# Attention and feed-forward stack: x loaded first, weights in pieces, v's products by key block, last transposes in another bank

## The chip, the cores and the metric

One core of one Trainium2 chip runs the whole program. The metric is the device time of one execution in microseconds, the median of several runs. A profiled execution of the same program gives the trace from which all rows below are taken; its times count from the start of its span. Engines: PE (TensorE, with PEld for its weight loads), DVE (VectorE), ACT (ScalarE), POOL (GpSimd), SP (SyncE).

## The reference, cut

Two layers on x of 16 sequences, 512 tokens, 256 features. The change touches only the first attention, with 16 heads of 64 features and windows of 128 tokens that look one window back and one forward:

```python
qkv = x @ w_qkv
q, k, v = jnp.split(qkv, 3, axis=-1)
...
q = l2norm(q) * q_scale
k = l2norm(k) * k_scale
...
bq = bq * jnp.cos(qf) + rotate_half(bq) * jnp.sin(qf)
bk = bk * jnp.cos(freqs) + rotate_half(bk) * jnp.sin(freqs)
...
sim = jnp.einsum('bwid,bwjd->bwij', bq, bk)
sim = jnp.where(window_mask, NEG, sim)
attn = jax.nn.softmax(sim, axis=-1)
out = jnp.einsum('bwij,bwjd->bwid', attn, bv)
...
return out @ w_out
```

After it come a layer norm, an int8 linear layer, a second attention without softmax, and a feed-forward block with ternary weights; all of that is one later stage, the layers, which the change does not touch.

## The kernel before

A setup block (`setup_attention`) runs first, and every engine waits at its end. It loads the projection weights of 6144 columns in two chunks of 3072, forms for each a high part (`whi`, ACT) and a low part (`wlo`, POOL for chunk 0, DVE for chunk 1), and builds the rotary tables `cos` and `sin` on DVE from `trig`, `q_scale` and `k_scale`, 32 small instructions. Then `run_attention` starts: SP loads x.

A sequence has 8 pairs of heads, and a pair has 4 windows, worked off in two halves (`u` is 0 or 1) of two windows each. Each engine runs `run_halves` over all 128 pairs in a fixed order written out by hand (`pe_half`, `act_half`, `dve_half`, `pool_half`), and semaphores tie the engines together. While pair n is in its softmax, PE projects pair n + 2 (`pe_project`: six matmuls per tile of 128 tokens, three products of high and low parts for each of two chunks of x, into `pj`), transposes q and k of pair n + 1 (`pe_q_transpose`, `pe_k_transpose`, bank `qk`), and makes the scores of the next windows (`pe_scores`, banks `sc`). DVE takes the masked maximum (L476), ACT the exponential (L381), POOL the normalized weights (L568). PE transposes these (`pe_transpose_weights`, L273): head 0 of the pair into bank `tp`, head 1 into `SC[0][0]`. ACT copies head 0 (L387) and DVE head 1 (L488) to `pt`. At the start of the next pair PE multiplies them with v into `qk` (`pe_values`, L283), once both copies of window 3 are there:

```python
e.wait_ge(g['pt_act'], NW * n + NW)
e.wait_ge(g['pt_dve'], NW * n + NW)
```

The bank `qk` is shared by the transposes of x, q and k, by v's products and by the out projection (L292), which happens in pair 0 of the next sequence. Projected q and k are rotated by DVE (L453 with cos, L455 with sin, reading the two halves of a head swapped), and added by POOL (L553); POOL then scales k by its norm (L560).

Of the kernel before, what the change touches and what calls it, by code (L numbers as in the profile page):

```python
# [99 lines left out]
def setup_attention(nc, io, mem):  # L100
    s = semaphores(nc, 'set1', 'load', 'late', 'hi_act', 'zero')
    arrived = [nc.alloc_semaphore(f'set1_wqkv{c}') for c in range(DC)]
    stages = [mem['weights'][:, :], flat(mem['ot'])[:, 0:3 * HD]]
    loads = [(mem['trig'], io['trig'].rearrange('(t p) k d -> p t k d', p=P)),
        (mem['q_scale'][:, :], broadcast_rows(io['q_scale'], DH)), (mem['k_scale'][:, :],
        broadcast_rows(io['k_scale'], DH))]

    def low_part(e, c):
        e.tensor_tensor(mem['wlo'][:, c, :], stages[c], mem['whi'][:, c, :].bitcast(F32), ALU.subtract)
    with nc.Block() as block:  # L110

        @block.sync
        def _(e):
            for c in range(DC):
                e.dma_start(stages[c], io['wqkv0'][:, c, :]).then_inc(arrived[c], 16)
            e.dma_start(mem['ident'][:, :], io['ident']).then_inc(s['late'], 16)
            e.dma_start(mem['wo'][:, :, :], io['wo0'].rearrange('(c p) n -> p c n', p=P)).then_inc(s['late'], 16)
            e.wait_ge(s['late'], 32)

        @block.scalar  # L120
        def _(e):
            e.preload_act_table_set('natural_log_exp_and_others')
            for dst, src in loads:
                e.dma_start(dst, src).then_inc(s['load'], 16)
            for c in range(DC):
                e.wait_ge(arrived[c], 16)
                e.activation(mem['whi'][:, c, :], stages[c], ACT.Copy).then_inc(s['hi_act'], 1)
            e.wait_ge(s['load'], 16 * len(loads))

        @block.gpsimd  # L130
        def _(e):
            e.memset(mem['mask'][:, :], 0.0).then_inc(s['zero'], 1)
            e.memset(mem['half'][:, :], -0.5).then_inc(s['zero'], 1)
            e.wait_ge(s['zero'], 2)
            prev, nxt = (mem['mask'][:, 0:WS], mem['mask'][:, 2 * WS:3 * WS])
            e.affine_select(out=prev, in_=prev, compare_op=ALU.is_ge, fill=MASKED, base=0, pattern=[[1, WS]],
                channel_multiplier=-1)
            e.affine_select(out=nxt, in_=nxt, compare_op=ALU.is_ge, fill=MASKED, base=0, pattern=[[-1, WS]],
                channel_multiplier=1)
            e.wait_ge(s['hi_act'], 1)  # L140
            low_part(e, 0)

        @block.vector
        def _(e):
            e.wait_ge(s['load'], 16 * len(loads))
            trig = mem['trig']
            for g, (gain, scale) in enumerate(((-Q_GAIN, mem['q_scale']), (1.0, mem['k_scale']))):
                for t in range(TT):
                    for h in range(2):
                        col = (2 * g + h) * DH  # L150
                        e.scalar_tensor_tensor(mem['cos'][:, t, col:col + DH], trig[:, t, 2 * g, :], gain,
                            scale[:, :], ALU.mult, ALU.mult)
                        swapped = scale[:, :].rearrange('p (s d) -> p s d', s=2)[:, ::-1, :]
                        e.scalar_tensor_tensor(mem['sin'][:, t, col:col + DH].rearrange('p (s d) -> p s d', s=2),
                            trig[:, t, 2 * g + 1, :].rearrange('p (s d) -> p s d', s=2), gain, swapped, ALU.mult,
                            ALU.mult)
            e.wait_ge(s['hi_act'], 2)
            low_part(e, 1)
# [1678 lines left out]
```

## Time and profile before

| | |
|---|---|
| runs, median (lowest to highest) | 3140.37 us (3139.62 to 3140.78), 3 runs |
| the profiled execution | 3136.01 us |
| its span, first to last instruction | 3134.2 us |
| PE busy | 2982.0 us, 95% |
| granted TensorE clock, mean of the span; tenths in 40 slices | 0.99; 9 in all but one, which has 7 |
| DVE, ACT, POOL busy | 2369.3, 2163.6, 1658.2 us |
| v's products (L283), first and last start | 62.9 and 1935.8 us |

The attention stage fills the time up to some 1940 us, the layers the rest. PE is the busiest engine, but a busy PE is not PE at its peak, since matmuls overlap in the record; what one costs is read from the start of one to the start of the next.

### The profile page before, as it was taken

The page shows a single profiled execution, that of the slowest core. Times are in us where ns is not written, and L with a number is a line of the kernel's source. Part 1 is how long each engine was busy: PE and PEld are TensorE (multiplying, and loading weights), DVE is VectorE, ACT ScalarE, POOL GpSimd, SP SyncE. Part 2 cuts the span into 40 slices and gives each one's busy share as a digit, 9 for nine tenths or more (in the row PEclk, how much of TensorE's full clock was granted, in tenths as well). Part 3 has the DMA queues.
Part 4 walks back from the last instruction along what each step waited for, and adds up shares of the span by engine and source line. Part 5 has one row for each costly group of instructions (what it writes and reads, how often), then busy time and mean ns, then how long its engine had stood idle before and what let it go on. Part 6 is the DMA issues. An engine that isn't in the chain of part 4 may idle for free. (4 is left out here: it accounts for less than half of the span.)

```text
span 3134.2 us, 62314 instructions
## 1 busy us (share of the span) xinstructions
PE 2982.0 (95%) x21167; PEld 2488.5 (79%) x21167; DVE 2369.3 (76%) x6867; ACT 2163.6 (69%) x5662; POOL 1658.2 (53%) x2222
## 2 busy tenths in 40 slices
PE   5999999999999999999999998699999999999996
PEld 4888888888888788788788886478888888888885
DVE  5877877877877877877877875687777777777775
ACT  4766765765765766766766765477888888888884
POOL 4655654654655655655655655334555555555555
PEclk9999999999999999999999999799999999999998
DMA  2000000000000000000000000200000000000000
GB/s 83 8 15 14 15 15 15 15 15 15 15 15 15 15 15 15 15 15 8 18 18 8 15 21 23 86 8 14 14 14 15 14 21 21 14 14 14 8 14 21
DMA packets 50058, 57.63 MB, mean 18 GB/s; under 512 B 2864, under 2 KB 47936, under 8 KB 49488
## 3 DMA queue, kind: packets, MB, share of 16 engines
q1 hardware_dynamic: 47072, 51.78, 5.3%
q8 instruction: 172, 2.82, 0.4%
q10 hardware_dynamic: 2672, 1.87, 0.2%
q14 instruction: 142, 1.16, 0.1%
HBM read 36.86 MB, written 16.78 MB: 17 GB/s over the span
## 5 line engine op out<-in xcount | busy, mean ns | idle before, releaser
L568 POOL TENSOR_SCALAR a_ex<-a_ex,a_rc 128x384 f32<-128x384 f32 (+1 forms) x1024 | 533.9, 536 | 716.6 <-DVE a_rc L483 716.6
L381 ACT ACTIVATE a_ex<-a_sm,a_nm 128x384 f32<-128x384 f32 (+1 forms) x1024 | 572.1, 560 | 62.8 <-DVE a_nm L476 50.5
L476 DVE CUSTOM_DVE_ANT_0 a_sm<-sc,a_mask,a_rn 128x384 f32<-128x384 f32 (+1 forms) x1024 | 530.9, 544 | 10.5 <-PE sc L262 10.5
L387 ACT ACTIVATE a_pt<-tp 128x256 f32<-128x256 f32 (+1 forms) x512 | 220.1, 430 | 310.4 <-PE tp L273 310.4
L231 PE MATMUL pj<-a_whi,a_xhi 128*128 128x384 f32 x1024 | 397.1, 388 | 2.0 <-DVE a_rb L455 1.7
L1599 POOL TENSOR_TENSOR b_alo<-b_ring,b_ahi 128x512 fp32r<-128x512 f32 x128 | 169.6, 1325 | 411.8 <-DVE b_ring L1428 375.2
L553 POOL TENSOR_TENSOR a_qr<-a_ra,a_rb 128x256 f32<-128x256 f32 x512 | 367.8, 733 | 24.8 <-DVE a_rb L455 22.2
L262 PE MATMUL sc<-a_kT,a_qT 64*128 64x384 f32 (+1 forms) x2048 | 345.2, 455 | 1.9 <-DVE a_pt L488 0.7
L231 PE MATMUL pj<-a_whi,a_xlo 128*128 128x384 f32 x1024 | 346.1, 338 | 0.0
L231 PE MATMUL pj<-a_wlo,a_xhi 128*128 128x384 f32 x1024 | 345.2, 337 | 0.0
L488 DVE COPY a_pt<-sc 128x256 f32<-128x256 f32 (+1 forms) x512 | 251.2, 491 | 90.3 <-PE sc L273 88.8
L283 PE MATMUL qk<-a_pt,a_v 128*64 128x128 f32 x5120 | 307.8, 274 | 10.9 <-ACT a_pt L387 0.9
L283 PEld LDWEIGHTS qk<-a_pt,a_v 128*64 128x64 f32 x5120 | 280.1, 137 | 47.1 <-issue 45.1
L262 PEld LDWEIGHTS sc<-a_kT,a_qT 64*128 64x128 f32 x2048 | 176.2, 186 | 95.3 <-issue 53.3
L453 DVE TENSOR_TENSOR a_ra<-pj,a_cos 128x256 f32<-128x256 f32 x512 | 214.7, 419 | 39.5 <-ACT a_sq L366 39.4
L273 PE MATMUL tp<-s_ident,a_ex 128*128 128x128 f32 x1280 | 228.6, 277 | 9.3 <-ACT a_pt L387 8.7
L273 PE MATMUL sc<-s_ident,a_ex 128*128 128x128 f32 x1280 | 230.5, 278 | 5.6 <-DVE a_pt L488 2.5
L292 PE MATMUL qk<-a_wo,a_ot 128*128 128x256 f32 x1024 | 228.0, 381 | 1.5 <-DVE a_res L496 0.8
L292 PEld LDWEIGHTS qk<-a_wo,a_ot 128*128 128x128 f32 x1024 | 192.0, 190 | 35.1 <-issue 8.2
L455 DVE TENSOR_TENSOR a_rb<-pj,a_sin 128x256 f32<-128x256 f32 x512 | 212.4, 415 | 0.0
L1395 DVE SCALAR_TENSOR_TENSOR b_ring<-k,b_one_bk,b_ring 128x512 f32<-128x512 f32 x128 | 95.9, 749 | 153.0 <-ACT b_ring L1259 149.6
L273 PEld LDWEIGHTS tp<-s_ident,a_ex 128*128 128x128 f32 x1280 | 152.2, 141 | 61.3 <-POOL a_ex L568 46.0
(229 smaller groups left out, 7946.5 us busy)
## 6 DMA issues: line engine op xcount, KB each, us to landing
a_xin<-x SPq DMA_DIRECT2D x16, 512.0 KB, 3.9
a_xres<-x SPq DMA_DIRECT2D x16, 512.0 KB, 3.9
y<-a_res SPq DMA_DIRECT2D x16, 512.0 KB, 2.9
b_y<-y SPq DMA_DIRECT2D x16, 512.0 KB, 3.8
out<-b_y SPq DMA_DIRECT2D x15, 512.0 KB, 2.9
a_xin<-wqkv SPq DMA_DIRECT2D x8, 256.0 KB, 2.7
a_pt<-wqkv SPq DMA_DIRECT2D x1, 1536.0 KB, 6.6
a_ot<-wqkv SPq DMA_DIRECT2D x1, 1536.0 KB, 10.5
```

The source lines that it names most:

```text
L231: last = e.matmul(PJ[t % 2][:, 0:3 * PW], a[:, c, t * P:(t + 1) * P], w[:, c, p * 3 * PW:(p + 1) * 3 * PW], start=c == 0 and k == 0, stop= ...
L262: e.matmul(SC[j][h][:, 0:width], qT[par][rows(h), (w + j) * WS:(w + j + 1) * WS], kT[par][rows(h), lo * WS:(hi + 1) * WS], start=True, sto ...
L273: last = e.transpose(TPS[h][:, k * P:(k + 1) * P], ex[h][w][:, k * P:(k + 1) * P], ident[:, :])
L283: last = e.matmul(QK[rows(h), w * WS:(w + 1) * WS], v[p % 4][:, k, rows(h)], pt[h][w][:, (k - lo) * P:(k - lo + 1) * P], start=k == lo, st ...
L292: last = e.matmul(QK[:, t * DIM:(t + 1) * DIM], ot[:, c, (2 * k + t) * P:(2 * k + t + 1) * P], wo[:, c, :], start=c == 0, stop=c == HC - 1)
L381: e.activation(ex[h][w][:, 0:width], sm[h][w % 2][:, 0:width], ACT.Exp, bias=nm[:, w, h:h + 1], scale=-1.0, accum_out=rs[:, w, h:h + 1]).t ...
L387: e.activation(pt[0][w][:, 0:width], TP[:, 0:width], ACT.Copy).then_inc(g['pt_act'], 1)
L453: e.tensor_tensor(ra[:, t % 2, :], qk, mem['cos'][:, t, :], ALU.mult)
L476: e.tensor_tensor_reduce(out=sm[h][w % 2][:, 0:width], in0=SC[w % 2][h][:, 0:width], in1=mem['mask'][:, off:off + width], scale=rn[:, par, ...
L488: e.tensor_copy(pt[1][w][:, 0:width], TPS[1][:, 0:width]).then_inc(g['pt_dve'], 1)
L553: e.tensor_tensor(qr[par][:, t, :], ra[:, t % 2, :], rb[:, t % 2, :], ALU.add).then_inc(g['rot_pool'], 1)
L568: e.tensor_scalar(row, row, 0.0, rc[:, w, h:h + 1], ALU.add, ALU.mult).then_inc(g['exn_pool'], 1)
```

## The change

Four things are changed.

1. The setup block is gone. Its work is done in `run_attention`, in the engines' own streams. SP loads x of sequence 0 in two halves first. The weights come in five pieces (of pairs 0, 1, 2 and 3, 4 and 5, 6 and 7), chunk 0 on SP's queue and chunk 1 on ACT's. High and low parts are made piece by piece: pieces 0 to 2 ahead of and among the first projections, pieces 3 and 4 in pairs 0 to 2. The second half of x is transposed into `tp`. The tables are two instructions; the rotation reads them by broadcast, and POOL's addition reads the swapped halves of `rb`.
2. v's products run over blocks of keys: per block and head one matmul of 256 or 384 columns, adding into the bank, in place of one of 128 columns per window and block. `pt` is laid out by key block, so the copies write blocks of 128 columns with a step.
3. The transposes of window 3, head 1, go to `qk` where `spare(i)` says so, in all pairs of a sequence but 0 and 6, and no longer wait for DVE's copy of window 2.
4. In the second half of a pair, except of pairs 0 and 6, the last six projection matmuls come in one run behind these transposes.

```diff
-    TPS = (TP, SC[0][0])
+    def spare(i):
+        pair, w = divmod(i, NW)
+        return w == 3 and pair % PAIRS not in (0, 6)
+
+    def tp_bank(h, i):
+        return TP if h == 0 else QK if spare(i) else SC[0][0]
...
+    def pt_keys(h, k):
+        lo, hi, width = span(k)
+        off = (lo - k + 1) * WS
+        return pt[h][:, k, off:off + width]
...
+    PIECES = [[0], [1], [2, 3], [4, 5], [6, 7]]
...
+    RAW_UNDER = {0: 3, 3: 4, 4: 5}
...
+    def act_weights_high(e, k):
+        e.wait_ge(w_in[k], 16 * DC)
+        for c in range(DC):
+            e.activation(whi[:, c, piece_columns(k)], w_raw[c][:, piece_columns(k)],
+                ACT.Copy).then_inc(g['wh_act'], 1)
...
     def pe_transpose_weights(e, i, w, h, follows):
         lo, hi, width = span(w)
         e.wait_ge(g['exn_pool'], 2 * i + h + 1)
-        if due(i):
+        if due(i) and not (h and spare(i)):
             e.wait_ge(g['pt_dve' if h else 'pt_act'], i)
-        if h and w % 2 == 0 and follows:
+        if h and spare(i):
+            seq, p = divmod(i // NW, PAIRS)
+            if due(i // NW):
+                e.wait_ge(g['ot_act'], i // NW)
+            if p == 5 and seq + 1 < B:
+                e.wait_ge(g['xl_dve'], 2 * (seq + 1) + 1)
+        elif h and w % 2 == 0 and follows:
             e.wait_ge(g['sm_dve'], 2 * (i + 2) + 1)
...
-        for w in range(NW):
-            lo, hi, width = span(w)
-            for k in range(lo, hi + 1):
-                for h in range(2):
-                    last = e.matmul(QK[rows(h), w * WS:(w + 1) * WS], v[p % 4][:, k, rows(h)],
-                        pt[h][w][:, (k - lo) * P:(k - lo + 1) * P], start=k == lo, stop=k == hi)
+        for k in range(NW):
+            lo, hi, width = span(k)
+            for h in range(2):
+                last = e.matmul(QK[rows(h), lo * WS:(hi + 1) * WS], v[p % 4][:, k, rows(h)], pt_keys(h, k),
+                    start=k == 0, stop=k == NW - 1, skip_group_check=True)
...
             pe_transpose_weights(e, i + 1, w + 1, 0, at.has_next())
-            if at.has_pair(2):
+            if at.has_pair(2) and p == 0:
                 pe_project(e, seq, n + 2, pair, w + 1, 0)
             pe_transpose_weights(e, i + 1, w + 1, 1, at.has_next())
+            if at.has_pair(2) and p:
+                pe_project(e, seq, n + 2, pair, w + 1, 0)
             if at.has_pair(2):
                 pe_project(e, seq, n + 2, pair, w + 1, 1)
...
-        e.activation(pt[0][w][:, 0:width], TP[:, 0:width], ACT.Copy).then_inc(g['pt_act'], 1)
+        e.activation(pt_window(0, w), blocks(TP, w), ACT.Copy).then_inc(g['pt_act'], 1)
...
-        e.tensor_tensor(qr[par][:, t, :], ra[:, t % 2, :], rb[:, t % 2, :], ALU.add).then_inc(g['rot_pool'], 1)
+        half = 'p (h s d) -> p h s d'
+        e.tensor_tensor(qr[par][:, t, :].rearrange(half, h=4, s=2), ra[:, t % 2, :].rearrange(half, h=4, s=2),
+            rb[:, t % 2, :].rearrange(half, h=4, s=2)[:, :, ::-1, :], ALU.add).then_inc(g['rot_pool'], 1)
...
-            for m in range(2):
-                for t in range(TT):
-                    for c in range(DC):
-                        pe_project(e, 0, m, m, t, c)
+            for m, t in [(0, 0), (0, 1), (0, 2), (0, 3), (1, 0), (1, 1)]:
+                for c in range(DC):
+                    pe_project(e, 0, m, m, t, c)
             pe_q_transpose(e, 0, 0, 0)
+            for c in range(DC):
+                pe_project(e, 0, 1, 1, 2, c)
             pe_k_transpose(e, 0, 0)
+            for c in range(DC):
+                pe_project(e, 0, 1, 1, 3, c)
             pe_scores(e, 0, 0, 0, 0)
```

PE at the end of a pair (here pair 1 of sequence 0, second half; `sc<-s_ident,a_ex` are the transposes of head 1, `tp<-s_ident,a_ex` those of head 0), before:

```order
121 L273 MATMUL sc<-s_ident,a_ex 128x128 x3
122 L273 MATMUL tp<-s_ident,a_ex 128x128 x2
123 L231 MATMUL pj<-a_whi,a_xhi 128x384
124 L231 MATMUL pj<-a_wlo,a_xhi 128x384
125 L231 MATMUL pj<-a_whi,a_xlo 128x384
126 L273 MATMUL sc<-s_ident,a_ex 128x128 x2
127 L231 MATMUL pj<-a_whi,a_xhi 128x384
128 L231 MATMUL pj<-a_wlo,a_xhi 128x384
129 L231 MATMUL pj<-a_whi,a_xlo 128x384
130 L283 MATMUL qk<-a_pt,a_v 64x128 x20
```

and the same place in the changed kernel:

```order
124 L309 MATMUL sc<-s_ident,a_ex 128x128 x3
125 L309 MATMUL tp<-s_ident,a_ex 128x128 x2
126 L309 MATMUL qk<-s_ident,a_ex 128x128 x2
127 L261 MATMUL pj<-a_whi,a_xhi 128x384
128 L261 MATMUL pj<-a_wlo,a_xhi 128x384
129 L261 MATMUL pj<-a_whi,a_xlo 128x384
130 L261 MATMUL pj<-a_whi,a_xhi 128x384
131 L261 MATMUL pj<-a_wlo,a_xhi 128x384
132 L261 MATMUL pj<-a_whi,a_xlo 128x384
133 L318 MATMUL qk<-a_pt,a_v 64x256 x2
134 L318 MATMUL qk<-a_pt,a_v 64x384 x4
135 L318 MATMUL qk<-a_pt,a_v 64x256 x2
```

The last two transposes moved ahead of three projection matmuls and into `qk`; eight wide matmuls of v's products stand in place of twenty narrow ones.

ACT at the very start, before:

```order
1 L122 ACT_TABLE_LOAD
2 L124 DMA a_res<-trig 128x4x256
3 L124 DMA a_q_scale<-q_scale 128x64
4 L124 DMA a_k_scale<-k_scale 128x64
5 L127 ACTIVATE a_whi<-a_pt 128x3072
6 L127 ACTIVATE a_whi<-a_ot 128x3072
```

and in the changed kernel:

```order
1 L708 DMA s_ident<-ident 128x128
2 L177 DMA a_ot<-wqkv 128x384
3 L711 DMA a_scales<-q_scale 128x64
4 L711 DMA a_scales<-k_scale 128x64
5 L712 ACT_TABLE_LOAD
6 L177 DMA a_ot<-wqkv 128x384
7 L177 DMA a_ot<-wqkv 128x768 x3
8 L399 ACTIVATE a_xhi<-qk 128x2x256
9 L399 ACTIVATE a_xhi<-tp 128x2x256
10 L182 ACTIVATE a_whi<-a_stage 128x384
11 L182 ACTIVATE a_whi<-a_ot 128x384
```

Eight DMAs now stand ahead of ACT's first activation, and that activation is of x and no longer of the weights.

## Rows read from the trace of the kernel before

**Rows 1.** The page, part 2: PE's busy tenths in 40 slices.

```profile
PE   5999999999999999999999998699999999999996
```

**Rows 2.** Timeline from 0 to 45: start us, duration us, engine, line, instruction, idle before.

```profile
7.35 2.76 ACT L127 ACTIVATE a_whi<-a_pt 128x3072 fp32r<-128x3072 f32 x1 [5.35 <-DMA a_pt<-wqkv]
10.20 6.67 POOL L109 TENSOR_TENSOR a_wlo<-a_pt,a_whi 128x3072 fp32r<-128x3072 f32 x1 [8.21 <-ACT a_whi L127]
...
16.31 0.64 DVE L151 SCALAR_TENSOR_TENSOR a_cos<-a_res,a_q_scale 128x64 f32<-128x64 f32 x1 [16.31 <-DMA a_k_scale<-k_scale]
...
21.07 3.34 DVE L109 TENSOR_TENSOR a_wlo<-a_ot,a_whi 128x3072 fp32r<-128x3072 f32 x1
24.68 0.37 SPq L610 DMA_DIRECT2D a_xin<-x  x1
...
28.61 1.12 PE L222 MATMUL qk<-s_ident,a_xin 128*128 128x128 f32 x4 [28.61 <-DMA a_xin<-x]
29.76 0.60 ACT L360 ACTIVATE a_xhi<-qk 128x512 fp32r<-128x512 f32 x1 [15.28 <-PE qk L222]
...
31.90 0.67 PE L231 MATMUL pj<-a_whi,a_xhi 128*128 128x384 f32 x1
```

**Rows 3.** Timeline of all engines from 39 to 49.

```profile
39.79 0.73 POOL L553 TENSOR_TENSOR a_qr<-a_ra,a_rb 128x256 f32<-128x256 f32 x1 [0.60 <-DVE a_rb L455]
41.62 1.05 POOL L560 TENSOR_TENSOR a_qr<-a_qr,a_rn 128x512 f32<-128x512 f32 x1 [1.10 <-ACT a_rn L372]
...
47.77 1.35 PE L262 MATMUL sc<-a_kT,a_qT 64*128 64x256 f32 x8 [0.69 <-ACT a_kT L376]
```

**Rows 4.** Timeline of PE from 62.5 to 63.2: the first of v's products.

```profile
62.93 0.51 PE L283 MATMUL qk<-a_pt,a_v 128*64 128x128 f32 x5
```

**Rows 5.** Timeline of PE, 1000 to 1053.

```profile
1004.70 7.07 PE L292 MATMUL qk<-a_wo,a_ot 128*128 128x256 f32 x32
...
1026.98 2.40 PE L283 MATMUL qk<-a_pt,a_v 128*64 128x128 f32 x40
1029.31 1.35 PE L262 MATMUL sc<-a_kT,a_qT 64*128 64x384 f32 x8
...
1038.31 0.34 PE L231 MATMUL pj<-a_wlo,a_xhi 128*128 128x384 f32 x1
1038.48 0.33 PE L231 MATMUL pj<-a_whi,a_xlo 128*128 128x384 f32 x1
1038.82 0.41 PE L273 MATMUL sc<-s_ident,a_ex 128*128 128x128 f32 x2
...
1039.41 0.34 PE L231 MATMUL pj<-a_whi,a_xlo 128*128 128x384 f32 x1
1039.83 2.40 PE L283 MATMUL qk<-a_pt,a_v 128*64 128x128 f32 x40
```

**Rows 6.** Timeline of DVE, 1036 to 1040.

```profile
1038.11 0.56 DVE L488 COPY a_pt<-sc 128x384 f32<-128x384 f32 x1 [0.38 <-PE sc L273]
...
1039.26 0.42 DVE L488 COPY a_pt<-sc 128x256 f32<-128x256 f32 x1
```

**Rows 7.** Timeline of ACT's queue, 1958 to 1970: the eighth issue of the layers' set-up.

```profile
1964.30 2.95 ACTq L1710 DMA_DIRECT2D b_gate<-gate  x1
```

**Rows 8.** Timeline of DVE, 1047.9 to 1053.1: the last gap before 1053.

```profile
1048.06 0.17 DVE L483 RECIPROCAL a_rc<-a_rs 128x2 f32<-128x2 f32 x1 [0.76 <-ACT a_ex L381]
```

**Rows 9.** The page, part 5: DVE's rotation, plain and swapped read (busy, mean ns, idle before).

```profile
L453 DVE TENSOR_TENSOR a_ra<-pj,a_cos 128x256 f32<-128x256 f32 x512 | 214.7, 419 | 39.5 <-ACT a_sq L366 39.4
...
L455 DVE TENSOR_TENSOR a_rb<-pj,a_sin 128x256 f32<-128x256 f32 x512 | 212.4, 415 | 0.0
```

**Rows 10.** Timeline of all engines from 1041 to 1043.6.

```profile
1041.42 1.54 POOL L553 TENSOR_TENSOR a_qr<-a_ra,a_rb 128x256 f32<-128x256 f32 x2
...
1043.45 0.33 PE L242 MATMUL qk<-s_ident,a_qr 128*128 128x128 f32 x1
```

**Rows 11.** Waits of PE, 60 to 2000: us in total, times, longest.

```profile
PE qk L249 <- DVE a_qT L468: 9.3, 16, 0.6
```

More of the change, by code:

```diff
@@ L98, in broadcast_rows @@
     return ap.rearrange('(a n) -> a n', a=1).to_broadcast([P, n])
[L100 to L113, printed above, removed]
-            for c in range(DC):
[L115 to L147, printed above, removed]
-                for t in range(TT):
-                    for h in range(2):
[L150 to L158, printed above, removed]
@@ L178, in rows, with pt_window, blocks @@
         return slice(h * DH, (h + 1) * DH)
+    def pt_keys(h, k):
+        lo, hi, width = span(k)
+        off = (lo - k + 1) * WS
+        return pt[h][:, k, off:off + width]
+    def pt_window(h, w):
+        lo, hi, width = span(w)
+        first = lo * 3 * WS + (w - lo + 1) * WS
+        return pt[h].rearrange('p k n -> p (k n)')[:, first:first + (hi - lo + 1) * 2 * WS].rearrange(
+            'p (k n) -> p k n', n=2 * WS)[:, :, 0:WS]
+    def blocks(bank, w):
+        lo, hi, width = span(w)
+        return bank[:, 0:width].rearrange('p (k n) -> p k n', n=WS)
     class Half:
@@ L202, in run_halves, with piece_columns, dma_piece @@
                     body(e, Half(b, p, u, b == 0, b == B - 1))
+    PIECES = [[0], [1], [2, 3], [4, 5], [6, 7]]
+    w_in = [nc.alloc_semaphore(f'att_w_in{k}') for k in range(len(PIECES))]
+    w_raw = [mem['stage'][:, :], flat(mem['ot'])[:, 0:3 * HD]]
+    def piece_columns(k):
+        return slice(PIECES[k][0] * 3 * PW, (PIECES[k][-1] + 1) * 3 * PW)
+    RAW_UNDER = {0: 3, 3: 4, 4: 5}
+    x_first = [nc.alloc_semaphore(f'att_x_first{k}') for k in range(2)]
+    def dma_piece(e, k, c):
+        e.dma_start(w_raw[c][:, piece_columns(k)], io['wqkv0'][:, c, piece_columns(k)]).then_inc(w_in[k], 16)
@@ new lines, in dve_tables, with pair_tables @@
+    def dve_tables(e):
+        e.wait_ge(g['scale_in'], 32)
+        e.wait_ge(g['trig_in'], 16)
+        scales = mem['scales'][:, :, :].rearrange('p k d -> p (k d)').unsqueeze(1).to_broadcast([P, TT, 2 * DH])
+        for j in range(2):
+            last = e.tensor_tensor(pair_tables(mem['rot'], j), pair_tables(mem['trig'], j), scales, ALU.mult)
+        last.then_inc(g['trig_dve'], 1)
+        e.wait_ge(g['trig_dve'], 1)
+    def pair_tables(t, j):
+        return t[:, :, 2 * j:2 * j + 2, :].rearrange('p t k d -> p t (k d)')
@@ L289, in pe_out_project @@
             e.wait_ge(g['op_dve'], 2 * seq + 1)
+        elif seq == 0:
+            e.wait_ge(g['wo_in'], 16)
         for t in range(2):
@@ L439, in act_half @@
                 act_project(e, n + 2, (p + 2) % PAIRS, w)
+        if at.first and (at.at(0, 0) or at.at(2, 0)):
+            act_weights_high(e, 3 + p // 2)
         if w1_piece(at) is not None:
@@ L545, in dve_half @@
             dve_rotate(e, n + 2, w)
+        if at.first and (at.at(0, 1) or at.at(2, 1)):
+            dve_weights_low(e, 3 + p // 2)
         if not at.first:
@@ L588, in pool_half @@
             norm.rstd(e, at.b - 1)
+        if at.first and (at.at(0, 1) or at.at(2, 1)):
+            pool_weights_low(e, 3 + p // 2)
         if w1_piece(at) is not None:
@@ L716, in attention_memory @@
     mem['weights'] = sb('pt', [P, 2 * NW * 3 * WS])
-    pt = mem['weights'][:, :].rearrange('p (h w n) -> p h w n', h=2, w=NW)
-    mem['pt'] = [[pt[:, h, w, :] for w in range(NW)] for h in range(2)]
+    pt = mem['weights'][:, :].rearrange('p (h k n) -> p h k n', h=2, k=NW)
+    mem['pt'] = [pt[:, h, :, :] for h in range(2)]
     for k, n in dict(sm=2, ex=4).items():
```

118 lines of the change are left out of this document (89 added, 29 removed).

## The prediction

> **What bounds the kernel now.** I read the page first. TensorE (PE) is busy for 95% of the span, by the table; the one thin place of the attention stage is the first slice, where PE stands at 5 tenths [rows 1]. So there are two questions: what fills the first slice, and what PE waits for in the repeating pairs of heads.
>
> The timeline of the start answers the first. Nothing multiplies until 28.61. The chain is: weights land, ACT makes the high part, POOL and DVE the low parts. DVE's second one starts at 21.07, because it is queued behind the rotary tables, whose k_scale came only at 16.31, and ends at 24.41. Only behind this block does SP issue the load of x (24.68), which lands 3.9 us later; projections begin at 31.90 [rows 2]. The first product of weights and v follows at 62.93, 31.03 us after the first projection [rows 4]. Within these 31 us PE transposes q of pair 0 only behind all eight projections, though POOL ended the last rotation of that pair at 40.52 (39.79 and 0.73) and began the norm of k at 41.62; the first scores start at 47.77 [rows 3].
>
> For the second question I take one pair, from its v products at 1026.98 to the next at 1039.83, 12.85 us. PE has hardly a gap. The start of each instruction against the next shows two: the last projection matmul ahead of the last transposes has 0.34 us (1038.48 to 1038.82) where its like take 0.17, and the last one ahead of the v products 0.42 (1039.41 to 1039.83) [rows 5]. Both wait on DVE's copies. DVE does the copy of window 2 (from 1038.11, after waiting for PE's transposes of that window), then a masked maximum and a reciprocal, and at once the copy of window 3 (1039.26, 0.42 us long, so to 1039.68) [rows 6].
>
> **The change part by part.**
>
> *Start.* The separate block goes. x is loaded first, in two halves, and the weights in five pieces. The queues start at about 0.7, and a load of x takes 3.9 us from issue to the first transpose (24.68 to 28.61); a half takes less, so its transposes run from about 3.5 to 4.6, and those of the second half to 5.7 (1.12 us each) [rows 2]. ACT has eight DMAs to issue ahead of its first activation. At SP's 0.37 us each, or half a microsecond, that ends at 3.7 to 4.7; but in the layers' set-up ACT has such a series too, and its eighth issue took 2.95 us [rows 7]. Free of that ACT starts its work on x at about 5, with it at 7.5. Then come two high parts of x (0.6 each), two high parts of 384 columns (2.76/8 and a start, 0.45 each), and the low part on DVE (3.34/8 and a start, 0.45) with POOL's (6.67/8, 0.83) beside it: 2.8 us in all. First projection at 7.9 to 10.5; I take 9.2, which is 22.7 us sooner than 31.90. Bounds: 7.5, if ACT waits for nothing, and 14, if the first pieces come nearly as late as k_scale does now.
>
> *The 31 us behind it.* Two pieces of the high and low parts now stand among the first pair's work. Piece 1 puts 0.9 us on ACT and POOL and 0.45 on DVE between projections; PE's own rhythm there is about 1.4 us per tile, so little shows. Piece 2 on ACT (1.7 us) lies under the norms of DVE, on POOL (1.7) ahead of the norm of k, which starts near 42.3 instead of 41.62 on the old scale. Against it, PE transposes q before its last two projections. The first scores then come about 1.8 us earlier than by the old distance of 15.87. Pieces 3 and 4 (1.5 us of ACT, 0.9 of DVE, 1.7 of POOL, each once) fall into pairs 0 to 2, where DVE has up to 0.76 us idle in a half pair [rows 8]; I charge a third of their 4.1 us, 1.3. Net -0.5 us, bounds -2 and +4.
>
> *v's products by key block.* Now 40 instructions of 128 columns take 2.33 us (1026.98 to 1029.31). The out projection, in one stream, takes 7.07 us for 32 of 256 columns, 0.216 each once the tail is off: two clock periods per column at 2.4 GHz, the level that the table's granted clock of 9 tenths and more stands for [rows 5]. By that rate 40 of 128 columns would take 4.3 us; they take half, so the two heads, in the two halves of the array's columns, run side by side and each pair of instructions takes 0.109. The change has 16 instructions of 256 or 384 columns: the same columns. 2 x (0.216 + 0.322 + 0.322 + 0.216) = 2.15 against 20 x 0.109 = 2.19. So 0.04 us a pair, 0.07 if the skew between the heads goes too; loads are hidden now as before. Not every pair passes it on: in pair 1 of each sequence, behind the out projection, PE waits 0.6 for DVE's copy of q anyway (9.3 us in 16 times), and in two more pairs of each eight DVE works without a gap from a place like 1048.06 to the end of the pair [rows 8, 11]. Five of eight, 80 pairs: 3.2 us; bounds 0 and 9.
>
> *Last transposes through the bank of q and k, projections in one run.* The wait at 1038.82 is on DVE's copy of window 2, which still reads the old bank. With another bank it goes, and six projection matmuls follow in a run. But the v products wait for DVE's copy of window 3, which ends at 1039.68 because of what DVE does before it, and none of that waits on these transposes [rows 6]. PE saves 0.16 us ahead of a wait that grows by 0.16. Worth 0; the cover is DVE's chain from 1038.11. The same holds where DVE is busy throughout.
>
> *Access patterns.* DVE's rotation reads the tables by broadcast and no longer in swapped halves, and both copies write blocks of 128 with a step. Now a swapped read costs 415 ns and a plain one 419 [rows 9], so I take 0, at most 0.01 each. POOL's addition reads swapped halves, which no row of POOL shows; the nearest, its product with a broadcast factor, takes 1.05 us for 512 elements, less per element than the plain addition's 0.73 for 256 [rows 3, 10]. I take 0.
>
> **Sum.** -22.7 - 0.5 - 3.2 = -26.4 us on an execution of 3136.0 (span 3134.2 and 1.8 around it), so 3109.6 there. That execution is 4.4 us under the median of the three runs, 3140.4; set against the median: 3114.
>
> **The rivals.** *The reorder pays.* If the copy of window 3 is not held by DVE's queue but by the transposes, 96 pairs get back 0.16 (0.3 in some): 15 to 22 us more, 3095. For it: PE does wait at both places. Against it: DVE's gapless rows. 10%.
>
> *The start pays less.* ACT's issues block until the pieces have landed, or the tables come late as k_scale does: first projection near 17, 7.5 us less, 3122. For it: the 2.95 us. Against it: x and the first pieces stand first in both queues. 12%.
>
> *POOL's swapped read is slow.* Two additions run from 1041.42 to 1042.96, and PE wants q at 1043.45 [rows 10]; 0.49 us are spare. Beyond 0.98 us per addition each pair loses twice the excess. The gain of 26 us is gone at 1.08 us; at double time (1.47) the kernel takes 3239 (2 x 0.49 x 128 = 125 more). Against it: the broadcast row. 4%. The Trainium skill ("GPSIMD Engine Reference", section 3.1) says that addresses are generated in hardware at no cycles; by it the addition stays as it is and this rival falls, but no row here shows that for a swapped read.
>
> *The two heads no longer run side by side* with 384 columns: 2.13 us a pair, 3387. Against it: the scores, whose two heads lie in the two halves of the rows, take 1.35 us, tail included, for 8 instructions of 256 and 384 columns, which only fits side by side [rows 5]. 2%.
>
> *Fewer instructions pay by themselves.* If an instruction's 0.058 us (2.33/40) were its own cost and not its columns', the 24 that go would save 1.4 us a pair, 178 in all: 2936. Against it: the out projection's 0.216 for twice the columns fits the columns alone [rows 5]. 1%. The Trainium skill ("TensorE: Matmul & The Clock Gate", section "Back-to-back issue gap") speaks for this rival: it has sustained pairs of load and matmul at about 81 ns for 128 columns and 131 ns for 512, by which 40 instructions would take 3.2 us and 16 wide ones, interpolated, 1.7, an estimate of 197 us in all. The row's 2.33 us for the 40 does not agree with it.
>
> **How the numbers follow.** My forecast, 3114 with its own range 3105 to 3119, has 71%. The range for 8 in 10 takes in the lesser start and most of the paying reorder: 3096 to 3123. A measurement tells no change to about 0.2%, 6 us. Faster: forecast, the rivals of the reorder and the start, and the last one, 0.94. Slower: POOL and serial heads, 0.05. Same 0.01.
>
> **What would show it.** First projection at 9.2 (7.9 to 10.5), first v products at about 40; v products 2.27 to 2.30 to the scores; pair 1 still 12.8 long, the wait at the last transposes gone and that ahead of the v products about 0.5 longer than the matmul; POOL's addition 0.73. Wrong, if pairs fall to 12.6 or less, if POOL's addition passes 0.98, or if ACT's first activation comes after 9.

## The result, and the profile after

| | before | after |
|---|---|---|
| median (lowest to highest), 6 runs of each | 3139.99 us (3136.19 to 3140.94) | 3115.87 us (3114.87 to 3117.91) |
| profiled execution, span | 3136.01, 3134.2 us | 3117.74, 3115.9 us |
| first projection, first scores | 31.90, 47.77 | 10.74, 27.80 |
| first v products, last v products | 62.93, 1933.65 | 44.95, 1916.43 |

The ratio is 0.9926 [0.9913, 0.9939]: 24 us less by the medians, where 26 were forecast from 3140.4. The two traces differ by 18.3 only: the execution before was 4.4 us under the median of its first three runs, the one after is 1.9 above its own. (The last v products' start is that of their first instruction.)

The page of the changed kernel, part 2 (tenths in 40 slices), beside [rows 1]:

```profile
PE   7999999999999999999999997699999999999996
PEclk9999999999999999999999999799999999999998
```

PE's first slice went from 5 to 7. The one other digit that moved, in slice 25 (8 to 7), is where the attention stage ends. The timeline of its start, beside [rows 2] (start us, duration us, engine, line, instruction, idle before):

```profile
2.69 4.84 SPq L177 DMA_DIRECT2D a_stage<-wqkv  x4
2.71 1.28 ACT L712 ACT_TABLE_LOAD   x1 [2.71 <-issue]
2.75 4.81 ACTq L177 DMA_DIRECT2D a_ot<-wqkv  x4
...
4.02 1.11 PE L247 MATMUL qk<-s_ident,a_xin 128*128 128x128 f32 x4 [4.02 <-DMA a_xin<-x]
...
7.61 0.60 ACT L399 ACTIVATE a_xhi<-qk 128x512 fp32r<-128x512 f32 x1 [3.61 <-issue]
...
8.58 0.53 ACT L182 ACTIVATE a_whi<-a_stage 128x384 fp32r<-128x384 f32 x1
...
9.18 1.00 POOL L187 TENSOR_TENSOR a_wlo<-a_stage,a_whi 128x384 fp32r<-128x384 f32 x1 [7.21 <-ACT a_whi L182]
9.55 1.05 DVE L187 TENSOR_TENSOR a_wlo<-a_ot,a_whi 128x384 fp32r<-128x384 f32 x1
...
10.74 0.66 PE L261 MATMUL pj<-a_whi,a_xhi 128*128 128x384 f32 x1 [4.22 <-DVE a_wlo L187]
```

x is transposed from 4.02, but ACT takes it up only at 7.61: its last four issues take 4.81 us. That is the blocked issue of [rows 7], which I had counted. DVE's low part takes 1.05 us and not 0.45: it runs beside POOL's and ends 0.42 after it (10.18 to 10.60).

The same view shows the projections slow at first:

```profile
16.01 0.52 PE L261 MATMUL pj<-a_wlo,a_xhi 128*128 128x384 f32 x1
...
16.60 0.34 PE L261 MATMUL pj<-a_whi,a_xhi 128*128 128x384 f32 x1
```

Up to 16.6 a projection matmul takes 0.52 us and starts 0.32 behind the last one; from there on it takes 0.34, at 0.17. The view by stretches has PEclk 1.00 from 11 to 16, but the clock's record in this trace begins only at 16.5, and the view counts time without a record as full. The 0.52 us is what these matmuls take further down, where the record has half. So these 5.9 us are by their durations at the lower level, 1.2 GHz. The kernel before has 3.0 us of it (31.90 to 34.90).

Further down the same view, around the first scores:

```profile
19.10 1.21 DVE L503 TENSOR_REDUCE a_ss<-a_sq 128x16 f32<-128x1024 f32 x1
...
19.95 1.82 POOL L187 TENSOR_TENSOR a_wlo<-a_stage,a_whi 128x768 fp32r<-128x768 f32 x1
...
20.34 1.46 DVE L506 TENSOR_SCALAR a_ss<-a_ss 128x16 f32<-128x16 f32 x1
...
23.58 0.69 PE L261 MATMUL pj<-a_whi,a_xhi 128*128 128x384 f32 x1 [2.58 <-DVE a_rb L498]
...
27.80 1.35 PE L292 MATMUL sc<-a_kT,a_qT 64*128 64x256 f32 x8
```

A DVE instruction of 16 columns takes 1.46 us, until POOL's low part of piece 2 ends. Behind it stands both engines' work for q and k, and PE waits 2.58. Pair 0 shows the same with piece 3:

```profile
47.92 1.79 POOL L187 TENSOR_TENSOR a_wlo<-a_stage,a_whi 128x768 fp32r<-128x768 f32 x1
...
49.19 0.56 DVE L506 TENSOR_SCALAR a_ss<-a_ss 128x16 f32<-128x16 f32 x1
...
49.68 0.72 POOL L598 TENSOR_TENSOR a_qr<-a_ra,a_rb 128x256 f32<-128x256 f32 x1
...
50.45 0.97 PE L272 MATMUL qk<-s_ident,a_qr 128*128 128x128 f32 x4 [1.86 <-POOL a_qr L598]
...
51.96 0.52 PE L261 MATMUL pj<-a_wlo,a_xhi 128*128 128x384 f32 x1
```

POOL's last rotation of pair 1 stands behind 1.79 us of low part, and PE waits 1.86 for it, for which there was no wait before. The matmuls behind it take 0.52 and not 0.34. The view by stretches (PEclk is the third number from the end) says why:

```profile
50.40:53.00 2.60, 2.55 (x11) 2.55 (x12) 1.51 (x5) 1.74 (x6) 1.05 (x1) 0.55 0.00 0
53.00:55.00 2.00, 2.00 (x14) 1.85 (x13) 0.77 (x4) 1.23 (x5) 0.00 (x0) 0.73 0.00 0
55.00:57.00 2.00, 2.00 (x15) 1.69 (x15) 1.52 (x7) 1.69 (x6) 1.72 (x4) 1.00 0.00 0
```

The granted clock fell to half, the lower level of 1.2 GHz, just behind the wait, for all but the first 0.3 us of the first stretch, and was back at 2.4 GHz in the middle of the second (0.73 of 2 us is half for 1.1). Pair 2 shows the same with piece 4: a wait of 1.94 us, and half clock behind it.

The end of a repeating pair, PE, beside [rows 5]:

```profile
1023.96 0.38 PE L309 MATMUL qk<-s_ident,a_ex 128*128 128x128 f32 x2
1024.10 0.42 PE L261 MATMUL pj<-a_whi,a_xhi 128*128 128x384 f32 x1
...
1025.06 0.33 PE L261 MATMUL pj<-a_whi,a_xlo 128*128 128x384 f32 x1
1025.58 0.98 PE L318 MATMUL qk<-a_pt,a_v 128*64 128x256 f32 x6 [0.19 <-DVE a_pt L530]
```

and DVE there, beside [rows 6]:

```profile
1023.94 0.56 DVE L530 COPY a_pt<-sc 128x384 f32<-128x384 f32 x1 [0.31 <-PE sc L309]
...
1024.95 0.16 DVE L525 RECIPROCAL a_rc<-a_rs 128x2 f32<-128x2 f32 x1
1025.03 0.41 DVE L530 COPY a_pt<-qk 128x256 f32<-128x256 f32 x1
```

The wait at the transposes is gone, and that ahead of the v products is 0.52 from start to start where it was 0.42 (I had it grow by 0.16). But the copy of window 3 starts 0.08 us behind the reciprocal. Before, it started 0.14 behind it (the reciprocal of 1039.12, the copy of 1039.26), just after the transposes of 1038.82, 0.41 long, had ended. So it did wait for them, by some 0.06 us.

Two groups of the page, and the waits of PE from 60 to 2000, answer to [rows 9, 10] and [rows 11]:

```profile
L598 POOL TENSOR_TENSOR a_qr<-a_ra,a_rb 128x256 f32<-128x256 f32 x512 | 369.3, 735 | 12.2 <-DVE a_rb L498 9.0
...
L498 DVE TENSOR_TENSOR a_rb<-pj,a_rot 128x256 f32<-128x256 f32 x512 | 212.2, 414 | 0.0
```

```profile
PE qk L318 <- DVE a_pt L530: 23.9, 96, 0.6
PE qk L279 <- DVE a_qT L510: 9.8, 16, 0.7
```

POOL's swapped read costs nothing (735 ns; 733 before), DVE's reads neither, and the wait for DVE's copy of q is what it was.

### The profile page after: what moved, and what is told of

It reads as the page before. It is cut to its first block and busy times, and to the rows that moved or that the text cites. A ratio compares the mean times of both kernels' runs of the same rounds, so it can differ in the third digit from the quotient of the medians.

```text
span 3115.9 us, 56168 instructions
## 1 busy us (share of the span) xinstructions
PE 2972.7 (95%) x18095; PEld 2381.2 (76%) x18095; DVE 2360.4 (76%) x6841; ACT 2164.3 (69%) x5670; POOL 1658.1 (53%) x2226
## 5 line engine op out<-in xcount | busy, mean ns | idle before, releaser
L318 PE MATMUL qk<-a_pt,a_v 128*64 128x384 f32 (+1 forms) x2048 | 303.9, 437 | 26.1 <-DVE a_pt L530 23.9
L318 PEld LDWEIGHTS qk<-a_pt,a_v 128*64 128x64 f32 x2048 | 158.4, 136 | 153.3 <-issue 60.4
L530 DVE COPY a_pt<-sc 128x384 f32<-128x384 f32 (+1 forms) x416 | 210.1, 505 | 85.3 <-PE sc L309 84.7
L497 DVE TENSOR_TENSOR a_ra<-pj,a_rot 128x256 f32<-128x256 f32 x512 | 214.6, 419 | 40.5 <-ACT a_sq L405 39.3
L498 DVE TENSOR_TENSOR a_rb<-pj,a_rot 128x256 f32<-128x256 f32 x512 | 212.2, 414 | 0.0
L261 PEld LDWEIGHTS pj<-a_whi,a_xhi 128*128 128x128 f32 x1024 | 195.3, 191 | 9.7 <-issue 4.7
L606 POOL TENSOR_TENSOR a_qr<-a_qr,a_rn 128x512 f32<-128x512 f32 x128 | 134.5, 1051 | 120.3 <-ACT a_rn L411 120.1
```

What stands on the lines that cost most here:

```text
L318: last = e.matmul(QK[rows(h), lo * WS:(hi + 1) * WS], v[p % 4][:, k, rows(h)], pt_keys(h, k), start=k == 0, stop=k == NW - 1, skip_group_c ...
L497: e.tensor_tensor(ra[:, t % 2, :].rearrange(heads, k=2, h=2), qk, rotary(t, 0), ALU.mult)
```

## The experiments

All were timed beside the kernel before on the same chip, whose medians there were 3136.6 (e1 to e4), 3137.9 (e5 to e8) and 3138.1 (e9, e10); the changed kernel's 3115.87 stood beside 3139.99. A difference of two medians from different groups is therefore good to some 4 us only, and the times inside the traces carry the finer readings. "Pairs" are the distances from one pair's v products to the next, read as starts in the timeline; "96 pairs" is the time from the first v products of sequence 2 to those of sequence 14.

| kernel | median us | ratio [95%] | first projection | first scores | first v products | pairs 0, 1, 2, 3 | 96 pairs |
|---|---|---|---|---|---|---|---|
| before | 3139.99 | | 31.90 | 47.77 | 62.93 | 12.82 12.86 12.83 12.83 | 1427.39 |
| changed | 3115.87 | 0.9926 [0.9913, 0.9939] | 10.74 | 27.80 | 44.95 | 16.25 13.54 16.31 12.71 | 1422.08 |
| e1 start only | 3121.94 | 0.9954 [0.9941, 0.9968] | 10.93 | 28.09 | 45.30 | 14.71 13.55 14.71 12.82 | 1427.22 |
| e2 old v products | 3118.58 | 0.9943 [0.9931, 0.9956] | 10.82 | 27.55 | 44.63 | 14.65 13.55 16.31 12.75 | 1423.56 |
| e3 bank, old order | 3115.76 | 0.9934 [0.9922, 0.9947] | 10.58 | 26.19 | 43.27 | 14.64 13.54 16.31 12.71 | 1421.92 |
| e4 high, low parts later | 3109.71 | 0.9916 [0.9903, 0.9930] | 10.75 | 25.07 | 41.71 | 12.73 12.71 12.71 12.73 | 1422.03 |
| e5 POOL's alone later | 3110.84 | 0.9911 [0.9897, 0.9924] | 11.10 | 25.55 | 43.47 | 13.40 13.57 13.49 12.71 | 1422.27 |
| e6 issues on SP | 3114.89 | 0.9924 [0.9911, 0.9938] | 9.33 | 26.42 | 43.48 | 14.64 13.53 16.32 12.73 | 1421.91 |
| e7 = e4 and e6 | 3106.26 | 0.9895 [0.9881, 0.9908] | 10.39 | 24.82 | 42.42 | 12.71 12.71 12.71 12.71 | 1422.09 |
| e8 order, old bank | 3148.07 | 1.0031 [1.0020, 1.0042] | 11.27 | 27.92 | 44.81 | 15.08 13.89 14.75 13.19 | 1447.36 |
| e9 = e7, low part on DVE | 3104.79 | 0.9894 [0.9879, 0.9910] | 9.00 | 25.58 | 42.22 | 12.71 12.70 12.72 12.71 | 1422.06 |
| e10 start, new v products | 3120.51 | 0.9946 [0.9934, 0.9959] | 11.02 | 27.45 | 44.51 | 16.33 13.55 14.74 12.80 | 1426.02 |

**The start alone (e1).** The changed kernel with the old loop of v's products, the old bank and the old order (the edits of e2, e3 and e8 together).

> The changed kernel with v's products per window, the bank and the order of before, so that only the start and the access patterns are new. The theory (the start pays 18 us at the first v products and loses 7 to 8 in pairs 0 to 2; products, bank and order give the rest in the repeating pairs) expects about 3125 us, 9 over the changed kernel, and repeating pairs as long as before, 12.82 us. The rival (the repeating pairs got faster by another thing, the patterns of DVE or POOL) expects them at 12.72 here too and some 3117.

Measured: 3121.94, and the 96 pairs are as before. The rotation's broadcast reads, POOL's swapped read and the copies' steps cost nothing in the repeating pairs; all that parts 2 to 4 bring lies between 3122 and 3116. The 3125 expected was 3 us too high. This trace has the start's stalls (PE waits 1.82 us in pair 0), but its granted clock stayed at 1.00 in pairs 0 to 2, and pairs 0 and 2 took 14.71 us where the changed kernel's took 16.3.

**Old v products (e2) and the products alone (e10).** e2 undoes part 2, with `pt` still laid out by key block:

```diff
-        for k in range(NW):
-            lo, hi, width = span(k)
-            for h in range(2):
-                last = e.matmul(QK[rows(h), lo * WS:(hi + 1) * WS], v[p % 4][:, k, rows(h)], pt_keys(h, k),
-                    start=k == 0, stop=k == NW - 1, skip_group_check=True)
+        for w in range(NW):
+            lo, hi, width = span(w)
+            for k in range(lo, hi + 1):
+                for h in range(2):
+                    off = (w - k + 1) * WS
+                    last = e.matmul(QK[rows(h), w * WS:(w + 1) * WS], v[p % 4][:, k, rows(h)],
+                        pt[h][:, k, off:off + WS], start=k == lo, stop=k == hi)
```

> The changed kernel with v's products per window of queries again (40 instructions of 128 columns), all else as changed. The theory (the columns cost, 0.03 us a pair is all that key blocks save) expects 2.33 us from the products to the scores and 2 to 4 us more in all. The rival (each instruction has a cost of its own) expects over 100 us more.

> The changed kernel with the last transposes in the old bank and the old order: start and v's products by key block alone. If the parts simply add (bank 3.7 us and products 1.5 over the 96 pairs of sequences 2 to 13): those 96 pairs take 1425.7, time 3120 to 3121. If the wider products only pay where the bank has taken the wait away (their 0.03 us a pair falls into the wait for DVE's copy): 1427, as with the start alone, time 3121.5 to 3122.5.

Measured: the wide products save 1.5 us of the 96 pairs in the new bank (1423.56 to 1422.08), 1.2 in the old (1427.22 to 1426.02). The parts nearly add, as the first case of e10 has it, and e2's 3118.58 is in its theory's 2 to 4 us. From v products to scores it is 2.30 us in the changed kernel and 2.33 before: the columns set the time, and not the number of instructions.

**The bank and the order (e3, e8).** e3 keeps the new bank and puts the order back (first piece); e8 keeps the order and puts the bank back (second):

```diff
-            if at.has_pair(2) and p == 0:
+            if at.has_pair(2):
                 pe_project(e, seq, n + 2, pair, w + 1, 0)
             pe_transpose_weights(e, i + 1, w + 1, 1, at.has_next())
-            if at.has_pair(2) and p:
-                pe_project(e, seq, n + 2, pair, w + 1, 0)
```

```diff
     def spare(i):
         pair, w = divmod(i, NW)
-        return w == 3 and pair % PAIRS not in (0, 6)
+        return False
```

> The changed kernel with the last projections in the order of before: three matmuls, the transposes of window 3, three matmuls. The bank stays new. The theory (what counts is only that the transposes no longer wait for the copy of window 2, since DVE takes up its copy of window 3 a fixed time after that of window 2) expects no difference to the changed kernel within 1 us: the transposes end at about 39.1 on the scale of before, ahead of DVE's reciprocal. The rival (the run of six matmuls itself pays) expects the pairs back at 12.80 and 6 us more.

> The changed kernel with the last transposes of head 1 back in the old bank, where they wait for DVE's copy of window 2, but with the six projection matmuls still in one run behind them. My theory (what these transposes wait for is DVE's copy, and the projections ahead of them filled this wait; in the new bank the order is free, in the old one it is not): PE idles ahead of the transposes, and v's products come 0.2 to 0.4 us later in each of 96 pairs: 20 to 35 us above the kernel without bank and order (some 3121), so 3140 to 3155. Rival (the order is free in either bank, since DVE's chain ends last): 3119 to 3123.

Measured: with the new bank the order is worth nothing (1421.92 against 1422.08). In the old bank it costs 21.3 us over 96 pairs against e10, a mean of 0.30 in the 72 that it touches: 0.37 to 0.38 in pairs 1, 2, 5 and 7 of a sequence, 0.14 in pairs 3 and 4. In e8, PE:

```profile
1038.93 0.41 PE L309 MATMUL sc<-s_ident,a_ex 128*128 128x128 f32 x2 [0.52 <-DVE a_pt L530]
...
1040.07 0.34 PE L261 MATMUL pj<-a_whi,a_xlo 128*128 128x384 f32 x1
1040.34 2.37 PE L318 MATMUL qk<-a_pt,a_v 128*64 128x256 f32 x16
```

and DVE:

```profile
1038.23 0.56 DVE L530 COPY a_pt<-sc 128x384 f32<-128x384 f32 x1 [0.37 <-PE sc L309]
...
1039.38 0.42 DVE L530 COPY a_pt<-sc 128x256 f32<-128x256 f32 x1
```

PE stands still for 0.52 us, then has all six projection matmuls still to do. DVE's copy ends at 1039.80, 0.54 us before v's products begin: here PE's own order sets the end, and no longer DVE. The three projections of the old order filled the wait for the bank. The new bank itself saves 0.04 to 0.09 us in pairs 1, 2, 5 and 7, and nothing in 3 and 4.

**The low parts behind q's and k's work (e4, e5).** e4 moves the low part of piece 2 behind the norm of k and pair 1's rotations on POOL and behind the last rotation on DVE. Of pieces 3 and 4 it moves the high parts on ACT into the next half pair, the low parts on DVE half a pair later, and those on POOL behind the first rotation of the next pair's second half (for piece 3 it starts 11.0 us behind the v products of pair 0, not 3.0). e5 moves POOL's alone, to the same places:

```diff
-            pool_weights_low(e, 2)
             pool_k_norm(e, 0, 0)
             for t in range(TT - 1):
                 pool_rotate(e, 1, 1, t)
+            pool_weights_low(e, 2)
...
+        if at.first and (at.at(1, 1) or at.at(3, 1)):
+            pool_weights_low(e, 3 + p // 2)
         if at.has_next():
...
-        if at.first and (at.at(0, 1) or at.at(2, 1)):
-            pool_weights_low(e, 3 + p // 2)
```

> The changed kernel with the making of the weights' parts at other places. Piece 2's low parts come behind the norm of k on POOL and behind the last rotation on DVE. Piece 3's and 4's high part comes one half pair later on ACT, behind the projection's copy; the low part on DVE half a pair later behind the copies, on POOL a pair later behind the first rotation of the second half. The theory (POOL's and DVE's low parts stand ahead of the last rotation and the norm of a pair, for which PE's transposes of q and k wait, and a small DVE operation waits until POOL's low part is done) expects pair 0 to 1 and 2 to 3 at 13 to 14 us in place of 16.3, the small operation at 0.18 us, and 5 to 8 us less in all. The rival (the loss there is from loads of wo, x and the pieces that arrive late) expects 16.3 as before.

> The changed kernel, with only POOL's low parts moved: piece 2 behind the norm of k and pair 1's rotations, pieces 3 and 4 half a pair later, into pairs 1 and 3. ACT's high parts and DVE's low parts stay where the change has them. In the kernel with all three engines' parts moved, pairs 0 to 2 took 12.7 us each and the time was 3109.7. Theory A (POOL's queue is what holds PE: the last rotation and k's norm stand behind 1.8 us of low part, and a small DVE instruction beside it waits for POOL's end): this kernel does the same, first five pairs 12.7 to 12.9, time 3109 to 3112, and the small DVE instruction at about 20 takes 0.17. Theory B (ACT's high parts ahead of q's and k's work and DVE's low parts cost as much): pairs 0 and 2 stay above 13.5, time 3112 to 3115.

Measured: e4 brings pairs 0 to 2 down to 12.7, as every later one, and has pair 3's v products 11.2 us sooner than the changed kernel (79.86, not 91.05); its time is 6 us less by the medians, 3 by the ratios. e5's is 5 us less, and pair 3 comes 7.1 sooner. Its small DVE instruction takes 0.17, and PE's wait in pair 0 is 0.30 and not 1.86. But its three pairs stay at 13.4 to 13.6, not the 12.7 to 12.9 that theory A wanted, so what ACT and DVE have in the way costs 0.7 to 0.9 in each. The fair measure is e1, whose clock stayed at full in these pairs: they take 42.97 us there, e5's 40.46, e4's 38.15. POOL's place is thus worth 2.5 us (some 0.3 of it the new bank and products, which e1 lacks) and ACT's and DVE's 2.3; in the changed kernel, whose three pairs take 46.10, the clock that fell behind POOL's stalls cost 3.1 more. Each theory has a part. In e4, DVE:

```profile
20.22 0.17 DVE L506 TENSOR_SCALAR a_ss<-a_ss 128x16 f32<-128x16 f32 x1
```

0.17 us again with no low part beside it, and the first scores come 14.3 us behind the first projection in place of 17.1 (e5 14.4). One loss stays in e4, the granted clock behind PE's wait of 2.3 us for the rotations of pair 1. The kernel before has the same wait, 2.27 us up to 53.51, and 1.00 behind it. In e4:

```profile
28.00:32.00 4.00, 1.73 (x12) 1.33 (x13) 2.94 (x8) 1.70 (x9) 3.00 (x7) 0.99 0.00 0
32.00:36.00 4.00, 4.00 (x20) 3.90 (x20) 2.49 (x10) 3.59 (x12) 1.92 (x3) 0.59 0.02 4
```

**ACT without the long issues (e6), and both (e7).** Pieces 1 to 4 of chunk 1 are issued on SP's queue:

```diff
                 dma_piece(e, k, 0)
+                if k:
+                    dma_piece(e, k, 1)
...
-            for k in range(1, len(PIECES)):
-                dma_piece(e, k, 1)
             for k in range(2):
                 act_x(e, 0, k)
```

> The changed kernel, with pieces 1 to 4 of chunk 1 issued on SP's queue behind chunk 0's, so that ACT has only four DMAs ahead of its first activation. Theory A (ACT's four last issues hold the start: x is transposed at 4.0 and ACT begins at 7.6): ACT's first activation at 4.6 to 5.5, first projection 2 to 2.5 us earlier, at 8.2 to 8.8, time 3113 to 3114.5 where the changed kernel has 3116. Rival (the pieces or the low parts are what is late: the first piece lands only at 7.5 or later, or pieces 1 and 2 come late because SP's own issues block): first projection within 0.7 us of 10.7, or the gain is lost again behind it, time 3115 to 3117.

> The changed kernel, with the issues of the run before on SP's queue and all low and high parts of pieces 2 to 4 moved later as in the run of the first job that did this. If the two effects add: first pairs 12.7 us, first v products at 39.2 to 40.2 in place of 44.9, time 3107 to 3108.5. If what ACT gains at the start is taken up again by late pieces: 3109 to 3110.

Measured, in e6:

```profile
3.73 2.10 SPq L177 DMA_DIRECT2D a_stage<-wqkv  x1
...
5.08 0.60 ACT L399 ACTIVATE a_xhi<-qk 128x512 fp32r<-128x512 f32 x1 [1.07 <-PE qk L247]
...
7.17 0.52 ACT L182 ACTIVATE a_whi<-a_stage 128x384 fp32r<-128x384 f32 x1
...
9.33 0.66 PE L261 MATMUL pj<-a_whi,a_xhi 128*128 128x384 f32 x1 [2.74 <-DVE a_wlo L187]
```

ACT begins 2.5 us sooner, as theory A has it; the long issues now stand on SP, where nothing waits behind them. But the first projection gains only 1.4, and the kernel's 1.0 is inside the noise: 9.33 and 3114.89 lie between the two theories. The second half of x (ACT waits 0.95 for it) and the low parts are next. In e7 it is the first piece itself:

```profile
8.23 0.52 ACT L182 ACTIVATE a_whi<-a_stage 128x384 fp32r<-128x384 f32 x1 [0.92 <-DMA a_stage<-wqkv]
```

e7 takes 3106.26, below what was expected and below the sum of the two effects (-6.2 and -1.0 would give 3108.7, but the intervals leave some 4 us). Its pairs are 12.71, but its first v products came at 42.42 and not at the 39.2 to 40.2 expected: the first projection came 1.1 later than in e6, and the granted clock was 0.66 from 28 to 32 and 0.50 from 32 to 36.

**Both first low parts on DVE (e9).** e7 with `weights_low(e, 0, 0, 'wl_pool')` in DVE's stream ahead of `dve_weights_low(e, 0)`, and POOL's `pool_weights_low(e, 0)` gone.

> The kernel e7_both_moved with one difference: DVE makes both low parts of piece 0, one behind the other, and POOL none. In e7 they run beside each other, 0.99 us on POOL and 1.04 on DVE, where DVE took 3.34 for 3072 columns, alone, in the kernel before (0.42 for 384). Theory A (the two slow each other down): each takes 0.42 to 0.55 on DVE, both are done 0.9 to 1.1 after the first starts, and the first projection comes 0.2 to 0.6 us earlier behind the first high part; time 3105.5 to 3106.5. Theory B (a low part takes 1.0 on DVE by itself): two take 2.1, the first projection comes 0.6 later, time 3106.5 to 3107.5.

```profile
7.14 0.52 ACT L182 ACTIVATE a_whi<-a_stage 128x384 fp32r<-128x384 f32 x1
...
7.83 0.55 DVE L187 TENSOR_TENSOR a_wlo<-a_stage,a_whi 128x384 fp32r<-128x384 f32 x1
...
8.29 0.55 DVE L187 TENSOR_TENSOR a_wlo<-a_ot,a_whi 128x384 fp32r<-128x384 f32 x1
...
8.99 0.66 PE L261 MATMUL pj<-a_whi,a_xhi 128*128 128x384 f32 x1 [2.44 <-DVE a_wlo L187]
```

Measured: theory A. Each takes 0.55, 0.46 from start to start, and the first projection comes 1.85 us behind the first high part, not 2.16 as in e6, e7 and the changed kernel. In the kernel's time 3104.79, below both ranges, cannot be told from e7. These two are the fastest of all: about 0.3% below the changed kernel.

The 1.4 us that e9 has over e7 at the first projection (8.99 and 10.39) are gone at the first scores, which come at 25.58, 16.6 us behind the first projection; in e7 it was 14.4. What differs is the slow level at the beginning:

```profile
17.99 0.52 PE L261 MATMUL pj<-a_whi,a_xhi 128*128 128x384 f32 x1
...
18.61 0.34 PE L261 MATMUL pj<-a_whi,a_xlo 128*128 128x384 f32 x1
```

The 0.52 us matmuls last 9.6 us here and 5.3 in e7. At half speed the 4.3 us more cost 2.2, an estimate that is just the difference of 16.6 and 14.4. Over all runs this stretch was 2.9 to 9.6 us long, and no run here shows what sets it.

## Why the prediction was right, and where not

The time, 3115.9 against 3114, lay in the range, and the likeliest case was the one that came. But luck had a part. The sum was -26.4 us for the execution that was profiled; between the two traces it was -18.3, 8 us less. The medians came out closer, at -24.1, because the profiled execution before was 4.4 us under the median that the forecast was set against, and the one after 1.9 above its own. Two terms were off, to opposite sides:

- **Start**, forecast -22.7: measured -21.2, first projection at 10.74 where I took 9.2 and allowed 10.5. The case of blocked issues was right (7.5 forecast, 7.61 measured). Of the 1.5 us over 9.2, 1.2 is that 9.2 stood halfway between issues that block and issues that do not. The other 0.3 is a size that failed, "the low part on DVE (3.34/8 and a start, 0.45) with POOL's (6.67/8, 0.83) beside it". They took 1.05 and 1.00, and all behind 7.61 took 3.13 us, not 2.8. DVE's waits for POOL's: e9 shows it, and saves 0.31. A shorter chain to x on ACT would have been worth 1.4 at the first projection (e6).
- **"The 31 us behind it"**, net -0.5 with bounds -2 and +4: measured +10.8, of which 1.2 up to the first scores, 2.0 from there to the first v products, and 7.6 in pairs 0 to 2. This is the step that failed. "Piece 2 on ACT lies under the norms of DVE, on POOL ahead of the norm of k" left out that DVE's small instruction stands still beside POOL's long one. And "I charge a third of their 4.1 us, 1.3" looked at DVE's idle time, while what counts is the work that stands behind the parts in each queue: on POOL 1.8 us in one piece ahead of the last rotation, for which PE waits. By e1, e4 and e5 the 7.6 are 2.5 of POOL's place, 2.3 of ACT's and DVE's and 3.1 of the clock, less the 0.4 by which e4's three pairs are shorter than those before. e4 brings the scores to where I had them (14.3 behind the first projection; 15.87 less 1.8 is 14.1).
- **The clock** had no term. It is some 6 of the 11.3 us by which the term above was off. Pairs 0 and 2 have 3.1 of it. Half clock from 33.6 to 37.0 is worth 1.7 of the 2.0 us between the first scores and the first v products, an estimate (e4, with such a stretch too, loses 1.5 there). The slow beginning, 5.9 us long and not 3.0, is worth 1.4 ahead of the scores, also an estimate. The same stall of pair 0 cost 3.4 us in the changed kernel (wait 1.86) and 1.8 in e3 (wait 1.85), by the lengths in the table. In e3 the clock stayed up, as its stretch behind the wait shows:

```profile
48.70:51.30 2.60, 2.53 (x19) 2.49 (x20) 1.86 (x6) 2.25 (x9) 1.07 (x2) 1.00 0.00 0
```

  Why it falls behind such a wait in one kernel's execution and not in another's is open.
- **v's products**, forecast -3.2: measured 1.2 to 1.5 us over 96 pairs, by proportion 1.6 to 2.0 over 128. Mechanism and places were right: between e1 and e10, by place in the sequence, the distances behind pairs 1, 4, 5, 6 and 7 fell by 0.02 to 0.03 us each, the others changed by less than 0.01. (In the new bank, e2 to the changed kernel, the one behind pair 1 fell by under 0.01 too.) The size was 0.024 and not 0.04.
- **Bank and order**, forecast 0: measured 3.7 to 3.9 us over 96 pairs (e1 to e2, e10 to the changed kernel), some 5 over 128. "None of that waits on these transposes" was wrong by 0.06 us: the copy of window 3 did wait for them. The cover was real for the rest: DVE's chain kept the other 0.1 of the 0.16, and the order alone pays nothing (e3). The rival of the paying reorder had the right place, but three to four times the size.
- **Access patterns**, 0: right (e1; POOL's 735 ns against 733). That rival fell, as did the two of serial heads and of the number of instructions.
- The layers behind, which no part of the change touches, took 1.1 us less in the trace. That is scatter: e1 to e10 show 1198.1 to 1202.3 there (1200.5 before).

Of the signs to look for, the 2.30 us of the v products, POOL's addition, and ACT's first activation ahead of 9 came as written, the wait at the last transposes went, and the repeating pairs stayed above 12.6. But pair 1 of sequence 0, where I had 12.8, took 13.54, and the first v products came at 44.95 and not at about 40.

## What to carry to other kernels

When one-time work is folded into a running schedule, look at each engine's queue for what stands behind it, not at the engine's idle time: with 1.8 us of POOL ahead of a rotation, and ACT's and DVE's parts ahead of theirs, a pair took 1.8 us more, or 3.4 where the granted clock fell behind the stall. With all of them behind that work it took nothing more. Where a bank is changed and an order with it, try them apart: the order that is free in the new bank costs a mean of 0.30 us a pair in the old. A sum that comes out right proves its terms only if each is checked by its own milestone.
